# Block A of a transformer layer on 8 cores: the rotary matmul of a projection chunk is issued one chunk later

## What is computed

```python
Q, K, V = (proj(wq, bq), proj(wk, bk), proj(wv, bv))      # x @ w.T + b
def rope(t):
    x1, x2 = (t[..., ::2], t[..., 1::2])
    t_rot = jnp.stack([-x2, x1], axis=-1).reshape(t.shape)
    return t * cos + t_rot * sin
Q, K = (rope(Q), rope(K))
...
gate = jax.nn.silu(x @ wg.T + bg)
```

## Time and profile before

| | us |
|---|---|
| median of 3 runs (6955.34 to 6968.92) | 6962.91 |
| profiled execution, its own time | 6949.71 |
| its slowest core, span | 6948.2 |
| spans of its eight cores | 6915.7 to 6948.2 |
| block A on core 0, from the first transposes to the last v group | about 165 to 1195 |

### The profile page before, as it was taken

The page is one execution under the profiler, slowest core; times in us unless marked ns, Lnnn a source line. Parts: engine busy times, 40 slices in busy tenths (PEclk is TensorE's granted clock), DMA queues, the critical chain, the costliest instruction groups (busy, mean ns, idle before and its releaser), DMA issues. The chain is left out here.

```text
span 6948.2 us, 87941 instructions; the slowest of 8 cores (6915.7 to 6948.2 us)
## 1 busy us (share of the span) xinstructions
PE 5082.5 (73%) x28608; PEld 2416.0 (35%) x28608; DVE 2748.9 (40%) x4527; ACT 2792.6 (40%) x3518; POOL 475.9 (7%) x916
## 2 busy tenths in 40 slices
PE   0666665888888888888888513478788888788887
PEld 0222222233332323332323101145455555455554
DVE  2333332363636454545454555632322222322223
ACT  0111111777787877777877410112112222122221
POOL 0000000520000000000000000011111111011110
PEclk9887887988899999899999756789889999899998
DMA  8445443970000000000000014356667777667776
GB/s 101 91 87 105 88 87 74 107 95 8 7 7 7 7 7 7 7 8 7 7 7 7 18 36 81 67 172 247 218 209 241 247 250 242 212 227 246 248 246 209
DMA packets 547640, 754.47 MB, mean 109 GB/s; under 512 B 323010, under 2 KB 372162, under 8 KB 546882
## 3 DMA queue, kind: packets, MB, share of 16 engines
q0 software_dynamic: 129712, 329.48, 17.3%
q1 hardware_dynamic: 137810, 350.03, 17.2%
q10 hardware_dynamic: 279680, 69.34, 5.8%
HBM read 698.17 MB, written 86.34 MB: 113 GB/s over the span
## 5 line engine op out<-in xcount | busy, mean ns | idle before, releaser
L650 PE MATMUL pOT<-big,vp 64*65 64x512 bf16 x4096 | 1323.3, 406 | 286.5 <-ACT big L719 143.5
L675 PE MATMUL S<-big,ktb 64*128 64x512 bf16 x4096 | 1308.2, 404 | 175.2 <-DVE big L712 95.9
L655 PE MATMUL pOT<-big,vp 64*65 64x512 bf16 x4096 | 1359.0, 415 | 0.0
L1272 PE MATMUL ph<-ktb,vp 128*128 128x256 bf16 x8192 | 1009.6, 278 | 16.0 <-DMA vp<-w_bf 15.1
L1312 PE MATMUL pz<-vp,ktb 128*128 128x512 bf16 x4096 | 968.7, 379 | 8.8 <-DVE ktb L1298 8.7
L1285 ACT ACTIVATE ktb<-ph,b_pp 128x256 bf16<-128x256 f32 x512 | 242.3, 473 | 1660.6 <-PE ph L1272 1660.6
L1272 PEld LDWEIGHTS ph<-ktb,vp 128*128 128x128 bf16 x8192 | 813.4, 100 | 241.9 <-issue 44.9
L696 ACT ACTIVATE big<-S 128x1024 bf16<-128x1024 f32 x768 | 763.2, 1022 | 273.0 <-PE S L675 183.1
L1295 DVE SCALAR_TENSOR_TENSOR ktb<-ktb 128x256 bf16<-128x256 bf16 x512 | 217.8, 425 | 1418.7 <-ACT ktb L1287 1418.7
L687 ACT ACTIVATE big<-S,big 128x1024 bf16<-128x1024 f32 x768 | 776.6, 1146 | 1.4 <-PE S L675 0.8
L712 DVE SCALAR_TENSOR_TENSOR big<-big,S 128x1024 f32<-128x1024 f32 x512 | 645.6, 1279 | 66.4 <-PE S L675 49.4
(11 more groups left out here) (157 smaller groups left out, 3027.2 us busy)
## 6 DMA issues: line engine op xcount, KB each, us to landing
vp<-w_bf SPq DMA_DIRECT2D x512, 512.0 KB, 4.5
vp<-w_bf POOLq DMA_DIRECT2D x512, 512.0 KB, 5.2
w_bf<-w POOLq DMA_DIRECT2D x256, 64.0 KB, 31.7
w_bf<-w POOLq DMA_DIRECT2D x64, 256.0 KB, 32.8
ktb<-ot_sc SPq DMA_DIRECT2D x64, 256.0 KB
out<-ktb SPq DMA_DIRECT2D x32, 512.0 KB, 2.7
big<-x POOLq DMA_DIRECT2D x32, 256.0 KB, 5.8
qt_sc<-big SPq DMA_DIRECT2D x64, 128.0 KB
```

The lines of the kernel that those rows point to most:

```text
L650: e.matmul(pOT[0][:, 512 * qh:512 * (qh + 1)], vp[0:64, kt, h, :], ptfin[0:64, par4, 512 * qh:512 * (qh + 1)], start=(kt == 0), stop=(kt = ...
L655: last = e.matmul(pOT[1][:, 512 * qh:512 * (qh + 1)], vp[64:128, kt, h, :], ptfin[64:128, par4, 512 * qh:512 * (qh + 1)], start=(kt == 0), ...
L675: last = e.matmul(Sp[par][:, 512 * qh:512 * (qh + 1)], ktb[r0:r1, pr_, 128 * kt:128 * (kt + 1)], qt_sb[r0:r1, gpar, 512 * qh:512 * (qh + 1 ...
L1272: last = e.matmul(ph[epar][:, 256 * hh:256 * (hh + 1)], w1e[:, slot, dc, 128 * hh:128 * (hh + 1)], xt2[:, dc, :], start=(dc == 0), stop=(d ...
```

## The change

The rotary part of a chunk is moved, unchanged, into a function `do_rot`. After the evacuation of a chunk has been appended, the chunk goes into a list `rot_pend`, and `do_rot` is called for the older of the two when there are more than one. What is left is appended after the eighth chunk. TensorE's queue then holds chain 0, chain 1, rotary 0, chain 2, rotary 1, ..., chain 7, rotary 6, rotary 7, for q and for k each. `chain_done` is still taken behind the last rotary matmul. No tile is added, and no instruction is added or removed. The g and v weights are as before (for g the list stays empty).

```diff
--- before.py
+++ after.py
@@ -366,6 +366,54 @@
             ci = 4 * tb + iw
             par = ci % 2
             if w in ("q", "k", "g"):
+                rot_pend = []
+
+                def do_rot(ec, qpar, t_ev, w=w, tb=tb, cpar=cpar):
+                    global_ns = None
+                    t_rot = P.op(
+                        "tensor",
+                        lambda e, qpar=qpar: e.matmul(
+                            pr[:, :], cb["cPerm"][:, :], qts[:, qpar, :],
+                            start=True, stop=True),
+                        waits=[t_ev, rot_state["pr_free"]], inc="mm")
+                    t_r1 = P.op(
+                        "vector",
+                        lambda e, cpar=cpar: e.tensor_tensor(
+                            rt1[:, :], pr[:, :],
+                            sinl[:, cpar, :], ALU.mult),
+                        waits=[t_rot, t_cs, rot_state["rt_last"]], inc="ve")
+                    rot_state["pr_free"] = t_r1
+                    t_r2 = P.op(
+                        "vector",
+                        lambda e, qpar=qpar, cpar=cpar:
+                        e.tensor_tensor(rt2[:, :], qts[:, qpar, :],
+                                        cosl[:, cpar, :], ALU.mult),
+                        waits=[t_ev, rot_state["rt_last"]], inc="ve")
+                    qts_free[qpar] = [t_r2]
+                    if w == "k":
+                        rt_l = P.op(
+                            "vector",
+                            lambda e, ec=ec, tb=tb: e.tensor_tensor(
+                                ktb[:, ec, 512 * tb:512 * (tb + 1)],
+                                rt1[:, :], rt2[:, :], ALU.add),
+                            waits=[t_r1, t_r2], inc="ve")
+                    else:
+                        dpar = ec % 2
+                        rt_l = P.op(
+                            "vector",
+                            lambda e, dpar=dpar: e.tensor_tensor(
+                                qtr[:, dpar, :], rt1[:, :], rt2[:, :],
+                                ALU.add),
+                            waits=[t_r1, t_r2, qtr_free[dpar]], inc="ve")
+                        P.dma(
+                            "dy",
+                            sc["qt"][128 * ec:128 * (ec + 1),
+                                     512 * tb:512 * (tb + 1)],
+                            qtr[:, dpar, :], waits=[rt_l])
+                        qtr_free[dpar] = P.mark("dy")
+                    rot_state["rt_last"] = rt_l
+
+                rot_state = {"pr_free": pr_free, "rt_last": rt_last}
                 for ec in range(8):
                     ppar = ec % 2
 
@@ -405,48 +453,13 @@
                               qts[:, qpar, :], waits=[t_ev])
                         qts_free[qpar] = [P.mark("dy")]
                     else:
-                        t_rot = P.op(
-                            "tensor",
-                            lambda e, qpar=qpar: e.matmul(
-                                pr[:, :], cb["cPerm"][:, :], qts[:, qpar, :],
-                                start=True, stop=True),
-                            waits=[t_ev, pr_free], inc="mm")
-                        t_r1 = P.op(
-                            "vector",
-                            lambda e, cpar=cpar: e.tensor_tensor(
-                                rt1[:, :], pr[:, :],
-                                sinl[:, cpar, :], ALU.mult),
-                            waits=[t_rot, t_cs, rt_last], inc="ve")
-                        pr_free = t_r1
-                        t_r2 = P.op(
-                            "vector",
-                            lambda e, qpar=qpar, cpar=cpar:
-                            e.tensor_tensor(rt2[:, :], qts[:, qpar, :],
-                                            cosl[:, cpar, :],
-                                            ALU.mult),
-                            waits=[t_ev, rt_last], inc="ve")
-                        qts_free[qpar] = [t_r2]
-                        if w == "k":
-                            rt_last = P.op(
-                                "vector",
-                                lambda e, ec=ec, tb=tb: e.tensor_tensor(
-                                    ktb[:, ec, 512 * tb:512 * (tb + 1)],
-                                    rt1[:, :], rt2[:, :], ALU.add),
-                                waits=[t_r1, t_r2], inc="ve")
-                        else:
-                            dpar = ec % 2
-                            rt_last = P.op(
-                                "vector",
-                                lambda e, dpar=dpar: e.tensor_tensor(
-                                    qtr[:, dpar, :], rt1[:, :], rt2[:, :],
-                                    ALU.add),
-                                waits=[t_r1, t_r2, qtr_free[dpar]], inc="ve")
-                            P.dma(
-                                "dy",
-                                sc["qt"][128 * ec:128 * (ec + 1),
-                                         512 * tb:512 * (tb + 1)],
-                                qtr[:, dpar, :], waits=[rt_last])
-                            qtr_free[dpar] = P.mark("dy")
+                        rot_pend.append((ec, qpar, t_ev))
+                        if len(rot_pend) > 1:
+                            do_rot(*rot_pend.pop(0))
+                while rot_pend:
+                    do_rot(*rot_pend.pop(0))
+                pr_free = rot_state["pr_free"]
+                rt_last = rot_state["rt_last"]
                 cos_used[tb] = P.tok("ve")
             else:
                 for ts_ in range(4):
```

## The result

The median of 9 runs of the changed kernel is 6810.9 us. Against the kernel before it is a ratio of 0.9778 (95% interval 0.9761 to 0.9796): 2.2% faster, some 155 us of 6963. In some executions of every kernel the cores of a die show a lower granted clock and the time is some per cent longer; the ratios in this text leave them out, the medians do not. The forecast was 6807.

A forecast was written before the change was run, and what follows sets the result against it. No engine fills block A; it consists of waits in turn. q falling to 19.1 and k to 15.25 us from 53.9 together saves 19.55 a token block, 156 for eight: 6949.7 gives 6794, plus 13.2 is 6807, range 6785 to 6841.

The forecast's parts named there:

- the hidden evacuations: In q and k, each 0.69 us evacuation lies under a 1.73 us chain, except before each stage's last rotary matmul.
- VectorE thus sets the pace: In q and k, VectorE's periods of 2.06 and 2.00 us lie just above TensorE's 1.94 and delay the last rotary matmul.
- q's stores are hidden: In q, the store the sixth sum needs lands at 17.1 us, VectorE reaches that sum at 17.6: 0.5 us to spare.
- 2.0 us are lost at q's slow start: q's first two chains take 5.45 us: 3.46 warm plus 2.0 lost to the low clock, a figure taken from g.
- The removed gap: In q and k, TensorE's waits for the evacuation, 120 of 1.09 us, and the last matmul's 0.17 us tail.
- k's second chain in the wait: k's second chain runs ahead of the rotary matmul, inside the wait for ScalarE's weight transfers: 1.73 us hidden.
- a clock of 0.5 beyond the first 5 us: Sign of a wrong prediction: granted clock of 0.5 inside q or k beyond their first 5 us.
- clock rivals: TensorE stays at 1.2 GHz through q and k, 6985, chance 0.02; or falls to 13/16 of its clock, 6840, chance 0.02.
- The level between: Rival: in q and k the die falls to 13/16 of its clock; about 123 us saved, 6840, chance 0.02.
- The rival of the two engines taking turns at PSUM: In q and k, r1 comes 0.69 us later each time, periods 2.75 and 2.69; 96 us saved, 6867, chance 0.05.
- The turn: Stretch from q's last rotary matmul to k's first, with its wait for ScalarE's weight transfers, taken as unchanged at 13.06 us.
- No gain by late weights: Rival: weight transfers are the true pace, k or g waits as much longer as the stage before is shorter; 6963, chance 0.03.

The follow-up runs named there:

- q or k alone: Kernel before with the rotary matmul delayed by one chunk in only one stage: q only, median 6917.4, ratio 0.9817; k only, 6940.2, ratio 0.9793.
- a dose of 0.8 us: Changed kernel with r2 done twice in every q and k chunk: median 6953.0 us, ratio 0.978; the same in the kernel before: ratio 1.0007.

## Where the prediction held, and where it failed

The time came out (6811 where 6807 stood), and so did the parts that carry it: the hidden evacuations, the chain inside k's wait, the rest of the kernel as before. Three steps of the working failed, and that their errors cancel in q is luck. *VectorE thus sets the pace*, with periods of 2.06 us in q and 2.00 in k: measured are 1.99 and 1.94, and in k it is TensorE that sets the pace. *q's stores are hidden*: they are not always. *2.0 us are lost at q's slow start*: it was 2.3.

*The removed gap* (120 waits of 1.09 us and the tail) went as worked out: q came to 19.2 us on the mean where 19.1 stood, k to 15.2 where 15.25 stood. The runs with q or k alone show that each stage earns its own half. The small difference in the sum lies on the side of before: the prediction took 53.9 us for both stages from two token blocks of core 0, the mean over the six cores was 53.4. So 19.1 us were saved a token block, not 19.55.

*k's second chain in the wait*: forecast 1.73 us a token block, measured 1.7 by putting it back.

*The clock*: 2.0 us lost at the start of a dense stretch, taken from g. In q the first rotary matmul came 5.8 us after the first chain's start on the mean (4.6 to 6.3), where 5.45 was forecast; the 4.82 of the token block shown above is one of the shortest. The prediction had as a sign of being wrong a clock of 0.5 beyond the first 5 us: in 40 of q's 48 stages the last matmul at the low level's pace ended later than that, 5.7 us after the start on the mean. In k the way from the first rotary matmul to the third took 6.0 us on the mean where 3.9 would be warm, 2.1 lost; in the rows below it took 6.5 (647.03 to 653.51), 2.6 lost. Neither of the clock rivals came: block A kept its 0.82, and chain and rotary matmul take 1.94 us, which is the full level's pace, on all eight cores. The level between did come in the experiments, with distances of 0.263 us for 0.216, a ratio of 0.82 near the 13/16 of the prediction. It came as well where only one stage was delayed, and not in the profile of the changed kernel; whether the change makes it more frequent is not shown.

```profile
647.03 0.59 PE L375 MATMUL pr<-big,cPerm_s 128*128 128x512 bf16 x1 [10.02 <-ACT big L442]
647.41 3.62 PE L423 MATMUL pq<-big 128*128 128x512 bf16 x8
650.83 0.63 PE L375 MATMUL pr<-big,cPerm_s 128*128 128x512 bf16 x1
651.25 2.42 PE L423 MATMUL pq<-big 128*128 128x512 bf16 x8
653.51 0.38 PE L375 MATMUL pr<-big,cPerm_s 128*128 128x512 bf16 x1
```

*VectorE's pace was over-sized.* The step took 0.17 us of idle ahead of r1, and 0.85 from r2 to the sum in q, as the earlier trace rows have it. VectorE's timeline after (core 6: two q chunks and the next r1, then a k sum and the next r1):

```profile
513.49 0.69 DVE L381 TENSOR_TENSOR big<-pr,big 128x512 bf16<-128x512 f32 x1
514.10 0.68 DVE L389 TENSOR_TENSOR big<-big 128x512 bf16<-128x512 bf16 x1
514.88 0.42 DVE L404 TENSOR_TENSOR big<-big 128x512 bf16<-128x512 bf16 x1
515.43 0.69 DVE L381 TENSOR_TENSOR big<-pr,big 128x512 bf16<-128x512 f32 x1
516.04 0.68 DVE L389 TENSOR_TENSOR big<-big 128x512 bf16<-128x512 bf16 x1
516.89 0.43 DVE L404 TENSOR_TENSOR big<-big 128x512 bf16<-128x512 bf16 x1 [0.17 <-DVE big L389]
517.42 0.69 DVE L381 TENSOR_TENSOR big<-pr,big 128x512 bf16<-128x512 f32 x1
...
769.11 0.42 DVE L396 TENSOR_TENSOR ktb<-big 128x512 bf16<-128x512 bf16 x1
769.66 0.69 DVE L381 TENSOR_TENSOR big<-pr,big 128x512 bf16<-128x512 f32 x1
```

The idle ahead of r1 is 0.10 us where VectorE is the later one (517.32 to 517.42) and 0.12 or 0.13 where it waits for TensorE. r2 to sum was read rightly: 0.85 for six of q's eight chunks, 0.79 for its first two and in k. So VectorE's own period is 0.61 + 0.85 + 0.43 + 0.10 = 1.99 us in q, and 0.61 + 0.79 + 0.42 + 0.10 = 1.92 in k. In q it falls 0.05 us behind TensorE's 1.94 with each chunk from the third on. TensorE shows nothing of it until the last rotary matmul, which comes 1.6 us after the one before it; by the evacuation alone it would be 1.26 (2.99 less the chain's 1.73). In k r1 follows r1 at TensorE's 1.94, with 0.02 us to spare, and the last rotary matmul comes 1.4 us after the one before it, since it waits for that one's r1 at the single `pr`. From q's first rotary matmul to its last the prediction had 13.65 us and the mean is 13.4. VectorE has next to no room left: a dose of 0.8 us lengthens the step from 1.94 to 2.78; smaller ones were not run.

The rival of the two engines taking turns at PSUM fell: of the 1024 r1s of the eight cores 812 ran while ScalarE evacuated a chain, and both kept their 0.69 us. ScalarE's row beside the r1 at 513.49:

```profile
513.25 0.69 ACT L442 ACTIVATE big<-pq,smal 128x512 bf16<-128x512 f32 x1 [1.25 <-PE pq L423]
```

The Trainium skill (PSUM — Partial Sum Buffer, Specifications) has it so for different banks. This trace agrees, for the two different tiles `pq` and `pr`.

*q's stores were called hidden, with 0.5 us to spare, and are not always.* In the sixth token block of the slowest core one sum waited for 3.96 us, and q took 23.7 us there:

```profile
736.39 0.68 DVE L389 TENSOR_TENSOR big<-big 128x512 bf16<-128x512 bf16 x1
741.02 0.43 DVE L404 TENSOR_TENSOR big<-big 128x512 bf16<-128x512 bf16 x1 [3.96 <-DMA qt_sc<-big]
```

This is the step that was wrong in kind: a mean pace of 2.3 us was taken for every store, and a single late one reaches TensorE through the sum, r1 and `pr`. It is small. The slowest core's sums waited for 8.3 us in all; over the six cores late stores held up TensorE's rotary matmuls in 3 of 48 stages, by 5.6 us together, 0.12 a stage. In the q shown first, one of the three, a short slow start (0.6 under the forecast) and a late store (0.7) make up for each other, and its 19.19 is no proof of the 19.1. On the mean, q's slow start (0.3 over) stands against the rest of q (0.2 under, late stores included).

*The turn* was taken as unchanged and is 0.4 us longer (13.2 to 13.6), 3 us in all. *No gain by late weights*: all chains together waited at most 5.9 us for weights on any core, in all of block A, and those were first chains of q. Block A became 153 us shorter on the mean of the cores, 156 were forecast. The mean span of the eight fell by 148, the slowest core's by 139 only: what follows block A took 5766 us on it against 5755 on the slowest core before, 5749 against 5745 on the mean of the eight. Why, the runs don't say.

What is still open: how much a late store costs the whole run, when the level between is granted, and how short g would be if its stores went as fast as on SyncE's queue.

## What to carry to other kernels

Where one engine's queue holds a short instruction that waits for another engine's treatment of the work just done, move it one piece of work back and count the next engine's period to a few hundredths of a microsecond: it tells whether all of the wait is won and how much room is left. Look at which pieces of work then come to stand ahead of a longer wait that stays; they are won besides. Then look for a queue that issues transfers ahead of computing work: here moving those took 105 us more off block A, two thirds of what the change did. And before a mean over cores is read, look at the pace of each: in three profiles here some cores ran at another clock level than the rest, which looked like an effect of the edit.

## What the runs showed of the hardware

A VectorE instruction (r1) that waits for the sum directly before it started 0.10 to 0.13 us after its end; q's sum, which waits for r2 and from the third chunk on for a store too, idled 0.17 behind r2, k's sum 0.11. The loss to the low clock level at the start of a dense stretch was not one number: 1.4 us in the q shown above (4.82 us for two chains that take 3.46 warm), 2.0 in g, 2.6 in the k shown above, and 1.2 to 2.8 over q's 48 stages; behind an idle of 0.88 us it was nothing. Between the low and the full level TensorE ran at a third one on some cores (128x512 matmuls 0.263 us apart; granted clock 0.81 where it is shown above). In the profile of k alone it was on cores 0, 1, 6 and 7, while cores 2 to 5, at the same time and with the same work, kept the full level. r1 and the evacuation, from two PSUM tiles at the same time, kept the 0.69 us that each takes alone.
